# Reordering the local attention layers: when ScalarE makes the norms and loads its second table, and where TensorE turns keys and makes the FFN products

## The reference, cut to what matters

```python
def attn_layer(x, Wqkv, qs, ksc, Wo):            # 16 heads of 64, windows of 32
    q, k, v = split(x @ Wqkv, 3); to heads
    q = l2norm(q) * qs; k = l2norm(k) * ksc
    q = q * cos * scale + rotate_half(q) * sin * scale
    k = k * cos / scale + rotate_half(k) * sin / scale
    out = local_attention(q, k, v)               # each window of 32 sees itself and the one before
    return out @ Wo
def ffn_layer(x, g, bln, W1, b1, W2, b2):
    xn = layernorm(x) * g + bln
    a, gate = split(xn @ W1 + b1, 2)             # 341 columns each
    return a * gelu(gate) @ W2 + b2
```

## Time and profile before

| what | value |
|---|---|
| median of 3 runs | 1280.44 us (1277.29 to 1285.11) |
| the profiled execution, its span | 1280.5 us |
| TensorE matmul busy | 1215.7 us (95%) |
| VectorE | 986.7 us (77%) |
| ScalarE | 938.3 us (73%) |
| POOL | 785.7 us (61%) |
| table loads L1966 and L1968 | 21 each, 1283 ns |
| chain that ended last | PE 46%, DVE 19%, ACT 18%, issue 11%, POOL 5% |
| instruction fetches in the DMA part | queue q8: 143 packets, 2.34 MB |

### The profile page before, as it was taken

How to read it: one execution, slowest core, us unless ns; L and a number is a source line. 1 busy time by engine, 2 the same in 40 slices (tenths; PEclk the granted TensorE clock), 3 DMA queues, 4 the chain that set the end, 5 groups by cost and what they waited for, 6 DMA issues and landing times.

```text
span 1280.5 us, 44796 instructions
## 1 busy us (share of the span) xinstructions
PE 1215.7 (95%) x17900; PEld 871.3 (68%) x17900; DVE 986.7 (77%) x2513; ACT 938.3 (73%) x2310; POOL 785.7 (61%) x805
## 2 busy tenths in 40 slices
PE   7999988999999999999999999999999999999996
PEld 5777745676767667767777677767677877777553
DVE  4666677888888788888888888888888656778677
ACT  6777775677777677777777777777777758788891
POOL 3444447878878787788777877778776102635000
PEclk9999998999999999999999999999999989999989
DMA  5000032222224322342225222422232001202000
GB/s 213 1 2 1 2 116 73 70 61 58 61 62 110 96 60 63 82 127 57 63 59 149 58 63 64 128 79 61 62 86 54 2 15 74 83 32 92 1 1 17
DMA packets 71743, 81.89 MB, mean 64 GB/s; under 512 B 15456, under 2 KB 63584, under 8 KB 71024
## 3 DMA queue, kind: packets, MB, share of 16 engines
q1 hardware_dynamic: 71536, 79.03, 22.4%
HBM read 31.22 MB, written 0.56 MB: 25 GB/s over the span
## 4 chain that ended last, share of the span: by engine, by line
PE 46%; DVE 19%; ACT 18%; issue 11%; POOL 5%; DMA 1%; SPq 0%; DVEq 0%; ACTq 0%; POOLq 0%
PE banks L823 3%; PE banks L808 3%; PE banks L391 2%; DVE arena L2862 2%; DVE arena L2861 2%; DVE small L2870 2%; PE banks L1143 2%; PE banks L1137 2%; PE banks L420 2%; DVE arena L2883 2%; DVE arena L2863 2%; DVE small L2871 2%; PE banks L1165 2%; PE banks L405 2%; PE banks L751 2%
## 5 line engine op out<-in xcount | busy, mean ns | idle before, releaser
L3998 POOL TENSOR_TENSOR arena<-arena,small 128x512 f32<-128x512 f32 x93 | 97.1, 1044 | 136.2 <-DVE small L2885 136.2
L1906 ACT ACTIVATE arena<-banks 128x512 f32<-128x512 f32 x94 | 56.1, 597 | 139.5 <-PE banks L759 139.3
L2861 DVE TENSOR_TENSOR arena<-banks,rotary 128x512 f32<-128x512 f32 x192 | 131.6, 685 | 22.7 <-ACT arena L1876 9.2
L3973 POOL TENSOR_TENSOR arena<-arena 128x512 f32<-128x512 f32 x96 | 122.7, 1278 | 26.3 <-DVE arena L2863 26.2
L808 PE MATMUL banks<-arena 64*64 64x32 f32 x5824 | 107.3, 221 | 15.5 <-issue 8.3
L3978 POOL TENSOR_TENSOR arena<-arena 128x512 f32<-128x512 f32 x95 | 121.4, 1278 | 0.2 <-DVE arena L2863 0.2
L607 POOL TENSOR_TENSOR arena<-arena,small 128x512 f32<-128x512 f32 x64 | 66.6, 1041 | 89.0 <-DVE small L534 89.0
L808 PEld LDWEIGHTS banks<-arena 64*64 64x64 f32 x5824 | 95.8, 135 | 27.0 <-ACT arena L1928 11.4
L3985 POOL TENSOR_TENSOR arena<-arena,small 128x512 f32<-128x512 f32 x95 | 99.5, 1047 | 5.6 <-ACT small L1916 5.6
L722 PE MATMUL banks<-slot,z 128*128 128x512 f32 x192 | 100.1, 603 | 1.3 <-DVE arena L2863 0.9
L3992 POOL TENSOR_TENSOR arena<-arena,small 128x512 f32<-128x512 f32 x95 | 99.2, 1044 | 0.0
(11 more groups left out here) (403 smaller groups left out, 3368.8 us busy)
## 6 DMA issues: line engine op xcount, KB each, us to landing
arena<-arena SPq DMA_DIRECT2D x576, 64.0 KB, 2.1
slot<-in_pack_dram SPq DMA_DIRECT2D x28, 339.5 KB, 3.4
arena<-arena SPq DMA_DIRECT2D x288, 32.0 KB, 1.9
slot<-in_pack_dram SPq DMA_DIRECT2D x2, 2713.5 KB, 9.2
slot<-in_pack_dram SPq DMA_DIRECT2D x1, 2693.5 KB
slot<-in_pack_dram SPq DMA_DIRECT2D x1, 2316.5 KB
arena<-gate_store SPq DMA_DIRECT2D x8, 256.0 KB, 3.9
slot<-in_pack_dram SPq DMA_DIRECT2D x4, 337.0 KB, 3.6
```

Of the source, the lines that this page charges most:

```text
L2861: e.tensor_tensor(rot, made, cos, ALU.mult)
L3973: e.tensor_tensor(m.rot_q[u % ROTS], m.rot_q[u % ROTS], m.sin_q[u % 2], ALU.add).then_inc(s["q_added"], 1)
```

## The change

TensorE's list gets a new order. The key turn moves from the end of the slot to between the turn of the weights and the scores. The last gate product moves from the end of its slot (remainder 0) to behind the value product of the next one (remainder 1). The FFN's output product moves from the end of its slot (remainder 2) to behind the query product of the next one (remainder 3), and its wait for the mask follows it. In `pe_scores` two waits change places.

On ScalarE the query copy stands behind the query square and ahead of exp. The norm of unit s is made in slot s + 1, behind that copy, and the norm of the last unit after the loop. The reload of natural_log_exp leaves `act_gelu` and becomes `act_tables`, behind the key copy and the output copy of the same slot.

On VectorE the last hidden product of the FFN stands ahead of the residual addition of its slot. On POOL the key's normalising stands ahead of `pool_lower` in every slot.

```diff
--- before.py
+++ after.py
@@ -763,9 +763,9 @@
 def pe_scores(e, s, m, u):
     lb, stage, b, t, half = unit_of(u)
     qT, kT = split(m.qT[u % 2], UP), split(m.kT[(lb % 2) * 2 + half], UP)
-    e.wait_ge(s["k_kept"], u + 1)
     if u >= OUT - SCORE:
         e.wait_ge(s["y_added"], u - (OUT - SCORE) + 1)
+    e.wait_ge(s["k_kept"], u + 1)
     if u:
         e.wait_ge(s["masked"], u)
     opened, renewed = done_by(u + SCORE, HIDE), done_by(u + SCORE, RENEW)
@@ -837,6 +837,8 @@
     for slot in range(LOCAL_SLOTS):
         if live(slot):
             pe_query(e, s, m, slot)
+        if ended(slot - 1, MERGE) is not None:
+            pe_ffn_out(e, s, m, ended(slot - 1, MERGE), slot - SCORE)
         if live(slot - TURN):
             pe_turn_query(e, s, m, slot - TURN)
         if live(slot - OUT):
@@ -845,6 +847,9 @@
             pe_gates(e, s, m, ended(slot, GATES))
         if live(slot):
             pe_value(e, s, m, slot)
+        if ended(slot - 1, GATE2) is not None:
+            pe_last_gate(e, s, m, ended(slot - 1, GATE2))
+        if live(slot):
             pe_key(e, s, m, slot)
         if slot == 0:
             e.wait_ge(s["x_done"], B)
@@ -855,6 +860,8 @@
             pe_centre(e, s, m, ended(slot, CENTRE))
         if live(slot - VALUE):
             pe_turn_weights(e, s, m, slot - VALUE)
+        if live(slot - TURN):
+            pe_turn_key(e, s, m, slot - TURN)
         if live(slot - SCORE):
             pe_scores(e, s, m, slot - SCORE)
         if live(slot - VALUE):
@@ -865,12 +872,6 @@
             pe_hidden(e, s, m, ended(slot, OPEN))
         if ended(slot, LAST) is not None:
             pe_last_hidden(e, s, m, ended(slot, LAST), min(slot - SCORE + 1, UNITS))
-        if ended(slot, GATE2) is not None:
-            pe_last_gate(e, s, m, ended(slot, GATE2))
-        if live(slot - TURN):
-            pe_turn_key(e, s, m, slot - TURN)
-        if ended(slot, MERGE) is not None:
-            pe_ffn_out(e, s, m, ended(slot, MERGE), min(slot - SCORE + 1, UNITS))
 
 
 def pe_end_turn_query(e, s, m, u):
@@ -1965,6 +1966,9 @@
     e.wait_ge(s["gate2_kept"], lb + 1)
     e.activation(m.gate[:, 0:2 * N], m.gate[:, 0:2 * N], ACT.Gelu)
     e.activation(m.gate[0:rows, 2 * N:3 * N], m.gate[0:rows, 2 * N:3 * N], ACT.Gelu).then_inc(s["gelued"], 1)
+
+
+def act_tables(e):
     e.preload_act_table_set("natural_log_exp_and_others")
 
 
@@ -1974,12 +1978,14 @@
             act_ln_end(e, s, m, ended(slot, RSTD))
         if live(slot):
             act_square_query(e, s, m, slot)
+        if live(slot - TURN):
+            act_query(e, s, m, slot - TURN)
+        if slot > RAMP:
+            act_norm(e, s, m, slot - 1)
         if live(slot - SOFT):
             act_exp(e, s, m, slot - SOFT)
         if ended(slot, KEEP2) is not None:
             act_last_gate(e, s, m, ended(slot, KEEP2))
-        if live(slot - TURN):
-            act_query(e, s, m, slot - TURN)
         if live(slot):
             act_value(e, s, m, slot)
             act_square_key(e, s, m, slot)
@@ -1997,12 +2003,13 @@
             act_key(e, s, m, slot - TURN)
         if live(slot - VALUE):
             act_out(e, s, m, slot - VALUE)
-        if live(slot) and slot >= RAMP:
-            act_norm(e, s, m, slot)
+        if ended(slot, GELU) is not None:
+            act_tables(e)
         if slot == 0:
             act_ln_square(e, s, 2 * B - 1, ln_views(m.ln_local), m.bank[FB])
         if slot == 1:
             act_ln_rstd(e, s, 2 * B - 1, ln_views(m.ln_local), m.bank[FB], m.eps)
+    act_norm(e, s, m, LOCAL_SLOTS - 1)
 
 
 def act_end_query(e, s, m, u):
@@ -2949,10 +2956,10 @@
             dve_renew(e, s, m, ended(slot, RENEW))
         if ended(slot, NORM) is not None:
             dve_xn(e, s, m, ended(slot, NORM))
+        if ended(slot, HIDE) is not None:
+            dve_last_hidden(e, s, m, ended(slot, HIDE))
         if live(slot - OUT):
             dve_residual(e, s, m, slot - OUT)
-        if ended(slot, HIDE) is not None:
-            dve_last_hidden(e, s, m, ended(slot, HIDE))
         if live(slot):
             dve_products(e, s, m, slot, 0)
         if live(slot - SOFT):
@@ -4023,10 +4030,10 @@
             pool_add_query(e, s, m, slot)
         if live(slot - 1) and slot <= RAMP:
             pool_norm_key(e, s, m, slot - 1)
+        if live(slot - 1) and slot > RAMP:
+            pool_norm_key(e, s, m, slot - 1)
         if live(slot - SCORE):
             pool_lower(e, s, m, slot - SCORE)
-        if live(slot - 1) and slot > RAMP:
-            pool_norm_key(e, s, m, slot - 1)
         if live(slot):
             stage = unit_of(slot)[1]
             if slot % (B * LAYER_UNITS) == B * LAYER_UNITS - 1 and stage < DEPTH:
```

## The result

The changed kernel takes 1242.7 us in the median of 4 runs (1237.93 to 1250.71), against 1282.78 for the kernel before in its 4 (1277.29 to 1286.73). The ratio is 0.970, with a 95% interval of 0.966 to 0.975. The profiled execution spans 1236.1 us, 44.4 less than the profiled one before.

The account below looks back on a forecast made before the run. TensorE's queue was taken to bound the kernel, local part 59% of the span. Terms -7.8 - 3.8 - 8 - 4 + 2 - 1.5 sum to -23.1 from 1280.44, giving 1257 us; own range 1249 to 1265, wider 1243 to 1272.

Parts of the forecast that it names:

- L751 for the key copy, slot 2: TensorE's query turn waits 0.49 for ScalarE's key copy in slots of remainder 2; this goes, 16 times: -7.8 us.
- L751 in slots 0 and 1, and a wide block after L808: Query-to-turn wait of 0.08 goes, some 47 slots: -3.8 us; a 128x512 product following L808 costs +2 us.
- L808 for the weights' copy: The moved key turn, 0.43, covers TensorE's 20 waits for ScalarE's copy of the turned weights: -8 us.
- L792 for POOL: POOL's earlier key normalising shortens 5 waits for normalised weights, delayed by new layers' rotary tables: -4 us.
- L808's stops ("I take 0"): TensorE's "issue" stops at L808, 8.3 us: taken as unchanged, since bursts keep their length; range -8 to +8.
- FFN output: TensorE's output product, 1.30 us, moves behind the query of slot 3; same work, so 0 us.
- ramp: First six slots: query copy no longer behind an exp that waits for POOL; between 0 and -4, taken -1.5 us.
- Nothing counted: ScalarE's new order of norm and query copy: its queue stays covered by TensorE's 4.4 us before weighted; 0 us.
- Returned by the instruction stream: TensorE without waits runs into more stops inside L781 and L808: +10 us, 1267; chance 0.15.
- Another wait takes the place: The key turn waits for the query copy in its own slot; half the gain or more lost: 1270 to 1282; chance 0.12.
- Slower: ScalarE's queue is late at L808 in every slot, some 40 us lost: 1297; chance 0.05.
- The table switch: Second table load costs twice its 1.28 us row, delaying slot 2's weighted product 0.5, 22 times: +11, 1268; chance 0.05.

Follow-up runs that it names:

- norm_back: The changed kernel with ScalarE's norm at the end of its own slot again: 1263.4 us.
- query_copy_back: The changed kernel with ScalarE's query copy behind norm, exp and last gate again: 1272.6 us.
- shifted changed kernel: The changed kernel with 32 small matmuls ahead of its first LayerNorm, which move positions in TensorE's instruction stream: 1247.1 us.

## Why the prediction was right in direction and too small

The terms of the sum, in the order of the prediction, with what the 89 slots show start to start in the two profiles:

| term | forecast | measured |
|---|---|---|
| L751 for the key copy, slot 2 | -7.8 | -9.2 |
| L751 in slots 0 and 1, and a wide block after L808 | -3.8 and +2 | +0.2 for both |
| L808 for the weights' copy | -8 | -9.3 |
| L792 for POOL | -4 | -4.0 |
| L808's stops ("I take 0") | 0 | -8.0 |
| waits for a layer's weights behind L808 | not seen | +2.8 |
| turns of queries and projections | not seen | -5.7 |
| turned weights, keys, last gate, variance | not seen | -4.2 |
| FFN output | 0 | -1.3, its last one now lies behind the stretch |
| ramp | -1.5 | -2.3 |
| drain | 0 | -3.5, by the clock |

*The waits* were read rightly, three of four within 1.5 us. The fourth, 0.08 in slots 0 and 1, was a wait as well: after the change query to turn takes 0.86 in slot 2, where no key turn and no L808 stands ahead of the query, and with the key turn put back it takes 0.94 again. What was mis-sized is the price set against it. In slots 0 and 1 the query now follows L808 and takes 0.96, so this price is 0.10 in some 44 slots, 4.4 us and not 2; it eats the whole of the 3.8 (which was itself counted over 47 slots where there are 44 or 45).

*The failed step* is the one on L808's "issue" stops, "I take 0, since neither burst gets shorter or longer". I looked at the length of the burst and not at when its instructions are fetched. They measured -8.0, at the very end of the range from -8 to +8 that the text gave them. And the same cause also defeats "Nothing counted" for ScalarE's new order: norm_back and query_copy_back show that the norm's and the query copy's places are worth 21 and 30 us once TensorE's order is the new one, mostly in stops that no wait names. What the runs showed in the step's place is that the stops go with the lead of the waits ahead of the burst; by which path is open. That the query copy must go ahead of exp was right; the price of leaving it, far more than a wait, was not in the text.

*Small lengths taken for the blocks' own.* 0.47 and 0.92 in the earlier trace rows were the tail of the wait ahead of them: 0.44 and 0.89 after. Each wait cost some 0.03 more in each of the two blocks behind it. The first four slots of the stretch, with no FFN over them yet, also had their own waits (31.1 us before, 27.6 after), on which I had not looked. And part is the clock: in the profile before, 5.8 us of the stretch lie at half of it (to 215.7, and from 430.7 to 434.1), where the query takes 1.7 and 1.5 us instead of 0.94; in the changed kernel's none does. Read from these rows that is some 2.6 us. All three are in the 9.9 us "not seen".

*The rivals.* "Returned by the instruction stream" had the right place and the wrong sign: fewer waits didn't make more stops, earlier grants went with fewer. "Another wait takes the place" and "Slower" name the query copy at the key turn; without ScalarE's part that case is real, but by stops and not by L808 waiting for L1928, so that the 1294.7 us measured lie near the 1297 written is luck. The table switch costs its 1.28 us and no more: L1972 starts at 399.44 and L1877 at 400.73.

*Slots.* 8.1, 7.9, 8.7 and 7.8 were drawn for remainders 3, 2, 1 and 0; the medians are 8.06, 7.70, 8.66 and 7.70.

## What to carry to other kernels

When an in-order engine works in dense bursts, look at how early its waits are granted, not only at whether it idles at them: grants just in time went with instruction fetches inside the burst and stops of up to 2 us each here. Look, too, at what "issue" stands for: here it was both such stops and waits for a layer's weights. Parts that only give each other cover can't be priced one by one. Alone, TensorE's, ScalarE's and POOL's parts are worth +12, -3 and -11 us; all without POOL's part -23, with it -40. And a block's length read next to a wait contains some of the wait; take it from a slot where nothing waits.

## What the runs showed of the hardware that was not expected

- TensorE's stops of up to 2.0 us move with the position in its stream by the fetch: 154 in 14 profiles, all on the same place of a block of 256 instructions, 140 of them in L808 (64 matmuls with their loads in 1.06 us). How many and how long they are goes with the lead of the waits ahead (table above, and 47 of 77 crossings with under 0.9 us against 14 of 156 with over 1.2). How far ahead of the array the sequencer can be was not measured, and which wait holds a fetch back is open.
- The key turn put back has no lead at L808 itself (0.05 in the median) and yet few stops, 5.9, of which 3.3 are waits for weights. The kernel before has the same 0.05 there and 11.4 without the weights; what differs is POOL's lead, 1.15 against 0.49. That this is why was not tested.
- An "issue" wait can be a DMA: the 27 at the first query of a layer each end 0.09 us after a landing of its weights.
- Stops also seem to cost clock: there are half-clock stretches of 3.4 us (1.2 GHz), 4 of them in the local part after the first six slots in query_copy_back and in norm_back each, 2 in the shifted changed kernel, and none in the profile of the changed kernel. In the kernel before, the stop of 1.68 us at 428.15 is followed by such a stretch from 430.7, in which the query product takes 1.50 us instead of 0.94.
- 32 matmuls at the kernel's start, where TensorE had only been waiting for data, cost 7 us: they ran for 9.2 us, and the first LayerNorm product began at 16.4 us instead of 7.4.
